# Expert slots of a mixture layer: first products two slots ahead, rows turned four ahead, slots rectified by ScalarE and VectorE in turn

## The chip, the core and the metric

The kernel runs on one core of one Trainium2 chip. The metric is the device time of one execution in microseconds (us). PE is TensorE, ACT ScalarE, DVE VectorE, POOL GpSimd, SP the engine that issues most DMAs.

## The reference

One transformer layer on x of 8 x 512 rows of 128 numbers, float32:

```
x = x + attention(layernorm(x), Wq, Wk, Wv, Wo, bo)      # 16 heads of 8, causal
h = layernorm(x).reshape(4096, 128)
probs = softmax(h @ gate_w.T)                            # 8 experts
topk_probs, topk_idx = top_k(probs, 2)
out_e = relu(h @ w1[e] + b1[e]) @ w2[e] + b2[e]          # 128 -> 512 -> 128
x = x + sum over the two chosen e of topk_probs * out_e
```

Only the two chosen experts of each row are needed.

## The kernel before, in words

Each engine has its own instruction stream, written out in full, and the streams meet at semaphores. Up to 350 us the kernel does attention, batch by batch (8 batches); beside it the finished batches are normalised a second time, routed, and scattered by POOL into `sorted_x`, a list in device memory that is sorted by expert in blocks of 128 rows.

From 350 us on the stage that is changed runs: 71 *slots* (`NSLOTS`), numbered 0 to 70. A slot is one block of 128 rows of one expert. The first 33 (`SLOTS[0]`) hold rows of batches that are routed already; slot 33 and later ones may hold rows of the last batches, whose scatters POOL issues between the slots (`SCATTERS6` in slots 1, 3, ... 13, `SCATTERS` in slots 15, 17, 18, 20, 21, 23, 24, 25). So the load of slot 33 waits until the scatter of slot 25 has landed. For slot i:

- SP: `load(i)` (L460) reads the block's number and brings the rows to `xs_t`, a ring of four (`ROUND`); it waits until PE has turned, and DVE has found the rows of, slot i-4.
- PE: `turn_xs(i)` (L1183, matmul L1187) transposes the rows into a PSUM bank; ACT: `copy_xs(i)` (L879) copies them to `xsT`; ACT: `copy_w1(i)` (L884) copies the expert's w1 to `w1_t`.
- PE: `expand(i)` (L1189, L1197), the first product, four matmuls 128x128x128 in float32; then `relu(i)`: ACT rectifies two of the four pieces (L890, L895), DVE the other two (L1737, L1743), into `hT`.
- PE: `contract(i)` (L1201, L1208), the second product, into `psO` or `psM` in turn (even and odd slots).
- DVE: `copy_y(i)` (L1747, L1750) adds b2 and writes `y_t` (named Qs in the profile); `find_rows` (L1752, L1756) works out where the rows go; POOL: `store_y(i)` (L692, L695) scatters them to `token_y` in device memory.

The order is written out by hand. In iteration i of the loops PE does expand(i+1), contract(i), turn_xs(i+3); ACT relu(i+1), copy_xs(i+3), copy_w1(i+3); DVE relu(i+1), copy_y(i), find_rows(i+2), then pieces of the last batch's attention and routing (`tail`) and weighted sums (`combine`). `xsT`, `w1_t` and `hT` have two places each, and expand uses two banks per slot, four in all. In the profile `turned` is xsT, `qrest` w1_t and `krest` hT. Near the end SP also loads results back in 512 KB pieces (`results_of`, L475 to L480), for the last two of which it waits until the scatter of slot 62 has landed; load(69) and load(70) are behind these on SP.

Of the kernel before, what the change touches and what calls it, by code (L numbers as in the profile page):

```python
# [13 lines left out]
P = 128  # L14
# [49 lines left out]
Y_RING = 8  # L64

# [77 lines left out]
def layer(nc, x, wq, wk, wv, wo, bo, gate_w, w1, b1, w2, b2, out):  # L143
    with ExitStack() as ctx:
# [134 lines left out]
        banks = [psT[:, 0, :], psT[:, 1, :], psT[:, 2, :], psS[:, 2, :]]  # L279
# [74 lines left out]
        def expert_reader(eng):  # L354
# [3 lines left out]
            def expert_of(i, at):  # L358
# [5 lines left out]
                if i not in experts:  # L364
                    experts.pop(i - 3, None)

                    experts[i] = eng.snap(words[k] // E ** (i - k * ROUND) % E, min_val=0, max_val=E - 1)
# [341 lines left out]
        def _(act):  # L709
# [169 lines left out]
            def copy_xs(i):  # L879
                act.wait_ge(xs_turned, i + 1)  # L880
                at_least(act, h_ready, i - 1)
                act.activation(xsT[:, i % 2, :], psS[:, 0, 0:P], ACT.Copy).then_inc(xsT_copied, 1)  # L882

            def copy_w1(i, e):  # L884

                at_least(act, h_ready, i - 1)
                act.activation(w1_t[:, i % 2, :], w1_sb[:, bass.ds(e, 1), :].rearrange("p a f -> p (a f)"), ACT.Copy)\  # L887
                    .then_inc(w1_copied, 1)

            def relu(i, e):  # L890

                act.wait_ge(h_ready, i + 1)
                at_least(act, y_ready, i - 1)
                for c in range(FC // 2):
                    last = act.activation(hT[:, i % 2, c * P:(c + 1) * P], banks[2 * (i % 2)][:, c * P:(c + 1) * P], ACT.Relu,  # L895
# [3 lines left out]
            act.wait_ge(moe_in, (1 + 2 * E) * 16)  # L899
            act.wait_ge(routed, 1)  # L900
# [3 lines left out]
            for i in range(2):  # L904
                copy_xs(i)
            relu(0, expert_of(0, 0))
            copy_xs(2)
            copy_w1(2, expert_of(2, 0))
# [19 lines left out]
        def _(pe):  # L928
# [254 lines left out]
            def turn_xs(i):  # L1183

                pe.wait_ge(xs_loaded[i % ROUND], (i // ROUND + 1) * 16)
                at_least(pe, xsT_copied, i)
                pe.transpose(psS[:, 0, 0:P], xs_t[:, i % ROUND, 0:D], identf[:, :]).then_inc(xs_turned, 1)  # L1187

            def expand(i):  # L1189
# [3 lines left out]
                at_least(pe, relu_act, i - 1)  # L1193
                at_least(pe, relu_dve, i - 1)
                for c in range(FC):
                    bank, c0 = banks[2 * (i % 2) + c // (FC // 2)], c % (FC // 2) * P
# [680 lines left out]
```

## Time and profile before

| | |
|---|---|
| time, median of 3 runs | 506.52 us (505.99 to 507.28) |
| span of the profiled execution | 527.7 us (no other time of that execution is given) |
| PE, PEld, DVE, ACT, POOL busy | 89%, 62%, 78%, 68%, 54% |
| chain that ended last, by engine | PE 50%, DVE 28%, ACT 7%, issue 7%, DMA 4% |
| slot stage | 350 to 516 us, then the last results and sums to 527.7 us |

PE is matmul work, PEld its weight loads, which lie beside it. A float32 matmul stands as two records, so the four matmuls of an expand are "x8" in a row. A timeline row has the start, the time from there to its end, the engine, line, operation, tiles and how many records it merges; in brackets the idle time of the engine before it and what ended it. "remote" is a semaphore event whose sender the profile could not name. The span is 21.2 us longer than the median time.

### The profile page before, as it was taken

What the parts mean: (1) busy time and instruction counts of PE and PEld (TensorE: products, weight loads), DVE (VectorE), ACT (ScalarE), POOL (GpSimd) and SP (SyncE); (2) the same over time, 40 slices, a digit from 0 to 9 for tenths busy, and PEclk for the clock granted to TensorE, in tenths of its full rate; (3) what the DMA queues carried; (4) which work ended last, traced back from release to release, by engine and by line L of the source; (5) the groups of instructions that cost most, each with busy time, mean ns of one, the idle gap of its engine ahead of it and who ended that gap; (6) DMA issues with size and microseconds to landing.
All of it is one profiled execution on the core that took longest, in us unless ns stands there. A gap on an engine that the chain in (4) does not pass through costs nothing.

```text
span 527.7 us, 14330 instructions
## 1 busy us (share of the span) xinstructions
PE 469.7 (89%) x4121; PEld 328.0 (62%) x4121; DVE 413.1 (78%) x1519; ACT 358.9 (68%) x782; POOL 286.6 (54%) x579
## 2 busy tenths in 40 slices
PE   3788999999999999999999999989788789999981
PEld 1545656556555545546555545459688679999980
DVE  6898878988988888888888897875556555557875
ACT  7576877777867867876866857875456457777750
POOL 5603544535755766657657565725456555545542
PEclk9879999999999999999999999999999899999997
DMA  7434232132233233233333326722222322235653
GB/s 225 134 93 129 56 118 91 56 118 88 67 120 108 70 108 110 76 101 97 102 95 98 106 76 175 209 65 63 56 63 69 85 77 74 71 79 180 182 172 101
DMA packets 49454, 54.92 MB, mean 104 GB/s; under 512 B 6564, under 2 KB 41554, under 8 KB 49377
## 3 DMA queue, kind: packets, MB, share of 16 engines
q1 hardware_dynamic: 44736, 45.18, 29.5%
q0 software_dynamic: 4320, 8.47, 4.7%
q8 instruction: 35, 0.57, 0.5%
q14 instruction: 43, 0.34, 0.2%
q10 hardware_dynamic: 320, 0.36, 0.2%
HBM read 34.96 MB, written 17.90 MB: 100 GB/s over the span
## 4 chain that ended last, share of the span: by engine, by line
PE 50%; DVE 28%; ACT 7%; issue 7%; DMA 4%; another core or an unknown queue 3%; ACTq 1%; SPq 0%; POOL 0%; DVEq 0%; POOLq 0%
PE psO L1035 12%; DVE psS L1349 10%; PE psT L1197 7%; DVE maxs L1352 7%; PE psS L998 7%; PE psM L1208 5%; PE psO L1208 5%; PE psT L1011 3%; PE psS L1197 2%; ACT PT L811 2%; DMA xs_t<-sorted_x 2%; PE psS L1187 2%; DVE maxs L1349 1%; DVE xn L1278 1%
## 5 line engine op out<-in xcount | busy, mean ns | idle before, releaser
L811 ACT ACTIVATE PT<-psT 128x512 f32<-128x512 f32 x320 | 172.5, 594 | 67.6 <-PE psO L1035 45.0
L1349 DVE CUSTOM_DVE_ANT_0 psS<-mask_row,psS 128x512 f32<-128x512 bf16 (+1 forms) x232 | 142.8, 624 | 33.6 <-PE psS L998 29.3
L998 PE MATMUL psS<-Ks,Qs 96*128 96x128 bf16 (+3 forms) x512 | 132.9, 308 | 9.5 <-DVE maxs L1352 7.3
L598 POOL TENSOR_SCALAR_AFFINE_SELECT PT<-PT 128x512 f32<-128x512 f32 x124 | 76.8, 635 | 96.0 <-ACT PT L811 94.8
L1011 PE MATMUL psT<-Qs,Ks 108*128 108x384 bf16 (+3 forms) x512 | 109.9, 299 | 4.2 <-ACT PT L811 3.0
L695 POOL DMA_INDIRECT token_y<-Qs,y_row x71 | 70.8, 997 | 74.6 <-DVE Qs L1750 39.0
L998 PEld LDWEIGHTS psS<-Ks,Qs 96*128 96x128 bf16 x512 | 50.4, 99 | 53.5 <-DVE maxs L1352 26.4
L629 POOL DMA_INDIRECT sorted_x<-xn,place x64 | 64.3, 1005 | 27.6 <-issue 16.5
L1352 DVE TENSOR_REDUCE maxs<-psS 128x2 f32<-128x512 f32 (+3 forms) x120 | 75.7, 669 | 1.8 <-PE psS L1001 1.4
L1035 PE MATMUL psO<-PT,Vs 128*32 128x512 f32 (+3 forms) x1024 | 75.8, 436 | 0.3 <-DVE x_all L1375 0.3
L1011 PEld LDWEIGHTS psT<-Qs,Ks 108*128 108x128 bf16 x512 | 43.5, 97 | 32.8 <-ACT PT L811 12.9
L1197 PE MATMUL psT<-turned,qrest 128*128 128x128 f32 x428 | 61.0, 280 | 1.3 <-ACT qrest L887 0.9
L895 ACT ACTIVATE krest<-psT,turned 128x128 f32<-128x128 f32 x142 | 44.7, 365 | 25.7 <-PE psT L1197 8.1
L1197 PEld LDWEIGHTS psT<-turned,qrest 128*128 128x128 f32 x428 | 54.1, 194 | 2.6 <-issue 2.5
L1035 PEld LDWEIGHTS psO<-PT,Vs 128*32 128x32 f32 x1024 | 28.6, 109 | 40.9 <-issue 27.4
L1001 PE MATMUL psS<-mask_row,identb 128*128 128x128 bf16 x280 | 49.9, 226 | 0.0
L887 ACT ACTIVATE qrest<-w_sb 128x512 f32 x71 | 44.6, 630 | 0.4 <-issue 0.4
L882 ACT ACTIVATE turned<-psS 128x128 f32<-128x128 f32 x71 | 19.7, 278 | 35.5 <-PE psS L1187 17.0
L1208 PE MATMUL psO<-w_sb,krest 128*128 x288 | 40.4, 285 | 3.4 <-ACT krest L895 2.3
L1208 PE MATMUL psM<-w_sb,krest 128*128 x280 | 38.2, 279 | 5.7 <-ACT krest L895 3.1
L1743 DVE TENSOR_SCALAR krest<-psS,turned 128x128 f32<-128x128 f32 x70 | 21.5, 347 | 23.0 <-PE psS L1197 12.1
L1208 PEld LDWEIGHTS psO<-w_sb,krest 128*128 128x128 f32 x288 | 36.6, 199 | 4.5 <-issue 4.4
(260 smaller groups left out, 741.1 us busy)
## 6 DMA issues: line engine op xcount, KB each, us to landing
Qs<-q_parts SPq DMA_DIRECT2D x96, 96.0 KB
Ks<-k_parts SPq DMA_DIRECT2D x95, 96.0 KB
xs_t<-sorted_x SPq DMA_DIRECT2D x71, 65.0 KB
w_sb<-in_L_ffn_w SPq DMA_DIRECT2D x16, 256.0 KB
k_parts<-kparts SPq DMA_DIRECT2D x8, 384.0 KB, 2.6
q_parts<-qparts SPq DMA_DIRECT2D x8, 384.0 KB, 3.6
x_all<-in_L_attn_x SPq DMA_DIRECT2D x8, 256.0 KB, 4.7
v_all<-token_y SPq DMA_DIRECT2D x4, 512.0 KB, 4.4
```

Of the source, the lines that this page charges most:

```text
L598: pool.affine_select(out=square, in_=square, compare_op=ALU.is_ge, fill=0.0, base=0, pattern=[[0, GH], [1, P]], channel_multiplier=-1).the ...
L629: pool.indirect_dma_start(out=xs_dram, out_offset=bass.IndirectOffsetOnAxis(ap=place[:, b, k, c:c + 1], axis=0), in_=xn2[:, b * CH + c, :] ...
L695: pool.indirect_dma_start(out=token_y, out_offset=bass.IndirectOffsetOnAxis(ap=y_row[:, i % (2 * Y_RING):i % (2 * Y_RING) + 1], axis=0), i ...
L811: act.activation(PT[:, n * T:(n + 1) * T], psT[:, bank, :], ACT.Exp).then_inc(prob_done[bank], 1)
L998: last = pe.matmul(psS[:, bank, c0:c0 + n], Qs[0:QK_ROWS, g, h, j * P:n], Ks[0:QK_ROWS, g, h, 0:n], start=True, stop=alone)
L1001: last = pe.matmul(psS[:, bank, c0 + n - P:c0 + n], identb[:, :], mask_qk[:, :], start=False, stop=True)
L1011: last = pe.matmul(psT[:, bank, c0:c0 + T - i * P], Ks[0:ST_ROWS, g, h, i * P:(i + 1) * P], Qs[0:ST_ROWS, g, h, i * P:T], start=True, stop ...
L1035: last = pe.matmul(psO[h * VW:(h + 1) * VW, i * P:T], Vs[:, g, i, h, :], PT[:, c0:c0 + cols], start=(i == KEY_BLOCKS[0]), stop=(i == KEY_B ...
L1197: last = pe.matmul(bank[:, c0:c0 + P], w1_t[:, i % 2, c * P:(c + 1) * P], xsT[:, i % 2, :], start=True, stop=True)
L1208: last = pe.matmul(ps_v[i % 2][:, 0:D], hT[:, i % 2, c * P:(c + 1) * P], w2_sb[:, bass.ds(e, 1), c, :].rearrange("p a d -> p (a d)"), star ...
L1349: dve.tensor_tensor_reduce(src, mask_row[:, (CH - 1 - j) * P:], src, 1.0, NEG, ALU.add, ALU.max, maxs[:, par, j, h:h + 1]).then_inc(scores ...
L1352: dve.tensor_reduce(maxs[:, par, j, h:h + heads], src, AX_X, ALU.max).then_inc(scores_used[bank], 1)
```

## The change

`expand` runs two slots ahead of `contract` instead of one, and `turn_xs` four ahead instead of three. `w1_t` and `hT` get three places (`DEEP`), in the memory of `qparts` and `kparts`; `xsT` gets four (`X_DEEP`), in that of `xn`. A slot's first product takes one whole bank of `psT` (three in turn) instead of two half banks of four; the turned rows use two banks in turn. Even slots are rectified by ACT alone and odd ones by DVE alone, four pieces each. The order of ACT's work in an iteration changes: copy_w1(i+3), relu(i+2) if i is even, copy_xs(i+4). DVE does relu(i+2) if i is odd, copy_y(i), find_rows(i+3). SP's and POOL's instructions are the same as before.

```diff
-        xsT = turned[:, E + E * FC:].rearrange("p (n d) -> p n d", n=2)
+        xsT = xn[:, 0, :, :]
-        w1_t = qrest
-        hT = krest
+        w1_t, hT = (v[:, :, :, :].rearrange("p u a t -> p (u a t)").bitcast(F32).rearrange("p (n f) -> p n f", n=DEEP)
+                    for v in (qparts, kparts))
-        banks = [psT[:, 0, :], psT[:, 1, :], psT[:, 2, :], psS[:, 2, :]]
+        xs_bank = [psS[:, 0, 0:P], psS[:, 2, 0:P]]
...
 # ACT
             def copy_xs(i):
                 act.wait_ge(xs_turned, i + 1)
-                at_least(act, h_ready, i - 1)
+                at_least(act, h_ready, i - X_DEEP + 1)
...
             def relu(i, e):
                 act.wait_ge(h_ready, i + 1)
-                at_least(act, y_ready, i - 1)
-                for c in range(FC // 2):
+                at_least(act, y_ready, i - DEEP + 1)
+                for c in range(FC):
...
-                if i + 1 < NSLOTS:
-                    relu(i + 1, expert_of(i + 1, i))
                 if i + 3 < NSLOTS:
-                    copy_xs(i + 3)
                     copy_w1(i + 3, expert_of(i + 3, i))
+                if i + 2 < NSLOTS and i % 2 == 0:
+                    relu(i + 2, expert_of(i + 2, i))
+                if i + 4 < NSLOTS:
+                    copy_xs(i + 4)
...
 # PE
             def turn_xs(i):
                 pe.wait_ge(xs_loaded[i % ROUND], (i // ROUND + 1) * 16)
-                at_least(pe, xsT_copied, i)
+                at_least(pe, xsT_copied, i - 1)
...
+            def rectified(i):
+                pe.wait_ge((relu_act, relu_dve)[i % 2], i // 2 + 1)
             def expand(i):
                 pe.wait_ge(xsT_copied, i + 1)
                 pe.wait_ge(w1_copied, i + 1)
-                at_least(pe, relu_act, i - 1)
-                at_least(pe, relu_dve, i - 1)
+                if i >= DEEP:
+                    rectified(i - DEEP)
...
-                if i + 1 < NSLOTS:
-                    expand(i + 1)
+                if i + 2 < NSLOTS:
+                    expand(i + 2)
                 contract(i, expert_of(i, i))
-                if i + 3 < NSLOTS:
-                    turn_xs(i + 3)
+                if i + 4 < NSLOTS:
+                    turn_xs(i + 4)
...
 # DVE
-                if i + 1 < NSLOTS:
-                    relu(i + 1, expert_of(i + 1, i))
+                if i + 2 < NSLOTS and i % 2:
+                    relu(i + 2, expert_of(i + 2, i))
                 copy_y(i, expert_of(i, i))
-                if i + 2 < NSLOTS:
-                    find_rows(i + 2)
+                if i + 3 < NSLOTS:
+                    find_rows(i + 3)
```

On PE, the begin of the slots up to the first contract; before (L1187 turns, L1197 expands, L1208 contracts; ISA rows compute addresses):

```order
L1187 MATMUL psS<-identf,xs_t 128x128 x2
L1197 MATMUL psT<-turned,qrest 128x128 x4
L1187 MATMUL psS<-identf,xs_t 128x128
L1197 MATMUL psT<-turned,qrest 128x128 x2
L1197 MATMUL psS<-turned,qrest 128x128 x2
L363 TENSOR_LOAD turns
L363 ISA x2
L1208 ISA
L1208 MATMUL psO<-w_sb,krest 128x128
```

and now (L1194 turns, L1207 expands, L1217 contracts):

```order
L1194 MATMUL psS<-identf,xs_t 128x128 x2
L1207 MATMUL psT<-xn,qparts 128x128 x4
L1194 MATMUL psS<-identf,xs_t 128x128
L1207 MATMUL psT<-xn,qparts 128x128 x4
L1194 MATMUL psS<-identf,xs_t 128x128
L1207 MATMUL psT<-xn,qparts 128x128 x4
L365 TENSOR_LOAD turns
L365 ISA x2
L1217 ISA
L1217 MATMUL psO<-w_sb,kparts 128x128
```

Three expands and four turns now stand ahead of the first contract, where there were two and three. From there on each iteration has the same three groups, one slot further on for expand and turn.

On ACT, one iteration inside the slots before (L882 copy_xs, L887 copy_w1, L895 rectify):

```order
L895 ISA
L895 ACTIVATE krest<-psT,turned 128x128
L895 ISA
L895 ACTIVATE krest<-psT,turned 128x128
L882 ACTIVATE turned<-psS 128x128
L887 ISA
L887 ACTIVATE qrest<-w_sb 128x512
```

and two iterations now (L884 copy_xs, L889 copy_w1, L897 rectify; `qparts` is w1_t, `kparts` hT, `xn` xsT):

```order
L884 ACTIVATE xn<-psS 128x128
L889 ISA
L889 ACTIVATE qparts<-w_sb 128x512
L884 ACTIVATE xn<-psS 128x128
L889 ISA
L889 ACTIVATE qparts<-w_sb 128x512
L897 ISA
L897 ACTIVATE kparts<-psT,turned 128x128
L897 ISA
L897 ACTIVATE kparts<-psT,turned 128x128
L897 ISA
L897 ACTIVATE kparts<-psT,turned 128x128
```

A fourth piece follows. The four pieces of an even slot stand ahead of the next copy_xs; in the other iteration ACT has the two copies alone.

## Rows read from the trace of the kernel before

**Rows 1.** Stretches (span, busy us of each engine with counts, granted clock, DMA share, GB/s).

```profile
386.00:418.00 32.00, 25.19 (x208) 23.56 (x207) 18.38 (x83) 17.09 (x52) 19.04 (x19) 1.00 0.27 75
430.00:505.00 75.00, 74.14 (x650) 72.95 (x649) 49.97 (x193) 55.13 (x153) 38.65 (x40) 1.00 0.39 110
```

**Rows 2.** Timeline of PE, one slot of the even stretch.

```profile
438.67 0.27 PE L1187 MATMUL psS<-identf,xs_t 128*128 128x128 f32 x1
...
439.67 1.06 PE L1208 MATMUL psO<-w_sb,krest 128*128 x8
440.56 0.27 PE L1187 MATMUL psS<-identf,xs_t 128*128 128x128 f32 x1
```

**Rows 3.** Timeline of all engines there: ACT, DVE and POOL.

```profile
443.78 0.63 ACT L895 ACTIVATE krest<-psT,turned 128x128 f32<-128x128 f32 x2 [0.18 <-PE psS L1197]
443.91 0.61 DVE L1743 TENSOR_SCALAR krest<-psS,turned 128x128 f32<-128x128 f32 x2 [0.72 <-PE psS L1197]
...
444.67 0.29 DVE L1750 TENSOR_TENSOR Qs<-psO,b_b 128x128 f32<-128x128 f32 x1
444.67 0.28 ACT L882 ACTIVATE turned<-psS 128x128 f32<-128x128 f32 x1 [0.26 <-PE psS L1187]
...
445.73 0.98 POOL L695 DMA_INDIRECT token_y<-Qs,y_row  x1 [0.91 <-issue]
```

**Rows 4.** Timelines of PE: contract(0), contract(25), and the turn of slot 33.

```profile
355.03 1.15 PE L1208 MATMUL psO<-w_sb,krest 128*128 x8 [0.19 <-issue]
...
423.33 1.15 PE L1208 MATMUL psM<-w_sb,krest 128*128 x8
...
436.69 0.27 PE L1187 MATMUL psS<-identf,xs_t 128*128 128x128 f32 x1
```

**Rows 5.** Timeline of all engines around contract(9).

```profile
375.63 1.13 PE L1197 MATMUL psT<-turned,qrest 128*128 128x128 f32 x8
...
378.78 0.63 ACT L895 ACTIVATE krest<-psT,turned 128x128 f32<-128x128 f32 x2 [3.75 <-remote]
378.93 0.61 DVE L1743 TENSOR_SCALAR krest<-psS,turned 128x128 f32<-128x128 f32 x2 [3.68 <-remote]
...
379.84 1.15 PE L1208 MATMUL psM<-w_sb,krest 128*128 x8 [3.08 <-ACT krest L895]
```

**Rows 6.** Stretch after that gap.

```profile
382.00:384.00 2.00, 2.00 (x11) 2.00 (x11) 0.80 (x3) 0.63 (x2) 1.49 (x2) 0.50 0.34 103
```

**Rows 7.** Timeline of all engines around contract(21).

```profile
409.71 0.61 DVE L1743 TENSOR_SCALAR krest<-psS,turned 128x128 f32<-128x128 f32 x2 [1.12 <-issue]
...
410.63 1.15 PE L1208 MATMUL psM<-w_sb,krest 128*128 x8 [1.16 <-issue]
```

**Rows 8.** POOL's last scatter, then a chain's DMA, SP's load(33), the first load and turn.

```profile
428.07 0.99 POOL L695 DMA_INDIRECT token_y<-Qs,y_row  x1 [1.82 <-DVE Qs L1750]
429.37 0.97 POOL L629 DMA_INDIRECT sorted_x<-xn,place  x1 [0.30 <-issue]
...
480.63 2.29 DMA token_y<-Qs,y_row
...
433.28 0.34 SPq L473 DMA_DIRECT2D xs_t<-sorted_x  x1
...
L473 SPq DMA_DIRECT2D xs_t<-sorted_x x71: 15/338/722, 349.4 to 505.9; - x71
...
351.30 0.30 PE L1187 MATMUL psS<-identf,xs_t 128*128 128x128 f32 x1 [0.35 <-DMA xs_t<-sorted_x]
```

**Rows 9.** End of contract(62) (next turn), load(70) in the chain, its turn, contract(70).

```profile
499.10 0.27 PE L1187 MATMUL psS<-identf,xs_t 128*128 128x128 f32 x1
...
505.94 4.92 DMA xs_t<-sorted_x
...
510.90 0.33 PE L1187 MATMUL psS<-identf,xs_t 128*128 128x128 f32 x1 [1.34 <-DMA xs_t<-sorted_x]
...
515.38 1.15 PE L1208 MATMUL psO<-w_sb,krest 128*128 x8 [0.39 <-issue]
```

More of the change, by code:

```diff
@@ L64 @@
 Y_RING = 8
+DEEP = 3
+X_DEEP = 4
 TAIL = dict(heads=0, norm=0, sorted6=1, attention=1, copy_attention=1, project=2, add=2, keep=4, best=4, second=5,
@@ L892, in relu @@
                 act.wait_ge(h_ready, i + 1)
-                at_least(act, y_ready, i - 1)
-                for c in range(FC // 2):
-                    last = act.activation(hT[:, i % 2, c * P:(c + 1) * P], banks[2 * (i % 2)][:, c * P:(c + 1) * P], ACT.Relu,
+                at_least(act, y_ready, i - DEEP + 1)
+                for c in range(FC):
+                    last = act.activation(hT[:, i % DEEP, c * P:(c + 1) * P], psT[:, i % DEEP, c * P:(c + 1) * P], ACT.Relu,
                                           bias=b1T[:, bass.ds(e * FC + c, 1)])
@@ L899, in _ @@
             act.wait_ge(moe_in, (1 + 2 * E) * 16)
+            act.wait_ge(q_stored[1], BATCH // 2 * Q_STORES)
+            act.wait_ge(k_stored[1], BATCH // 2 * K_STORES)
             act.wait_ge(routed, 1)
@@ L903, in _ @@
             copy_heads(STEPS - 1, GROUPS - 1)
-            for i in range(2):
+            for i in range(3):
                 copy_xs(i)
-            relu(0, expert_of(0, 0))
-            copy_xs(2)
-            copy_w1(2, expert_of(2, 0))
+                if i == 0:
+                    copy_w1(2, expert_of(2, 0))
+                if i == 1:
+                    relu(0, expert_of(0, 0))
+            copy_xs(3)
             for i in range(NSLOTS):
@@ L1185, in turn_xs @@
                 pe.wait_ge(xs_loaded[i % ROUND], (i // ROUND + 1) * 16)
[L1186 to L1187 removed]
+                at_least(pe, xsT_copied, i - 1)
+                pe.transpose(xs_bank[i % 2], xs_t[:, i % ROUND, 0:D], identf[:, :]).then_inc(xs_turned, 1)
+            def rectified(i):
+                pe.wait_ge((relu_act, relu_dve)[i % 2], i // 2 + 1)
             def expand(i):
@@ L1192, in expand @@
                 pe.wait_ge(w1_copied, i + 1)
-                at_least(pe, relu_act, i - 1)
-                at_least(pe, relu_dve, i - 1)
+                if i >= DEEP:
+                    rectified(i - DEEP)
                 for c in range(FC):
-                    bank, c0 = banks[2 * (i % 2) + c // (FC // 2)], c % (FC // 2) * P
-                    last = pe.matmul(bank[:, c0:c0 + P], w1_t[:, i % 2, c * P:(c + 1) * P], xsT[:, i % 2, :],
-                                     start=True, stop=True)
+                    last = pe.matmul(psT[:, i % DEEP, c * P:(c + 1) * P], w1_t[:, i % DEEP, c * P:(c + 1) * P],
+                                     xsT[:, i % X_DEEP, :], start=True, stop=True)
                 last.then_inc(h_ready, 1)
@@ L1203, in contract @@
                     pe.wait_ge(heads_copied, STEPS)
-                pe.wait_ge(relu_act, i + 1)
-                pe.wait_ge(relu_dve, i + 1)
+                rectified(i)
                 at_least(pe, y_copied, i - 1)
                 for c in range(FC):
-                    last = pe.matmul(ps_v[i % 2][:, 0:D], hT[:, i % 2, c * P:(c + 1) * P],
+                    last = pe.matmul(ps_v[i % 2][:, 0:D], hT[:, i % DEEP, c * P:(c + 1) * P],
                                      w2_sb[:, bass.ds(e, 1), c, :].rearrange("p a d -> p (a d)"),
@@ L1218, in _ @@
             turn_xs(2)
+            expand(1)
+            turn_xs(3)
             for i in range(NSLOTS):
@@ L1739, in relu @@
                 dve.wait_ge(h_ready, i + 1)
-                at_least(dve, y_ready, i - 1)
-                for c in range(FC // 2, FC):
-                    c0 = (c - FC // 2) * P
-                    last = dve.tensor_scalar(hT[:, i % 2, c * P:(c + 1) * P], banks[2 * (i % 2) + 1][:, c0:c0 + P],
+                at_least(dve, y_ready, i - DEEP + 1)
+                for c in range(FC):
+                    last = dve.tensor_scalar(hT[:, i % DEEP, c * P:(c + 1) * P], psT[:, i % DEEP, c * P:(c + 1) * P],
                                              b1T[:, bass.ds(e * FC + c, 1)], 0.0, ALU.add, ALU.max)
@@ L1835, in _ @@
             dve.wait_ge(routed, 1)
-            find_rows(0)
-            find_rows(1)
-            relu(0, expert_of(0, 0))
+            dve.wait_ge(k_stored[1], BATCH // 2 * K_STORES)
+            for i in range(3):
+                find_rows(i)
+            relu(1, expert_of(1, 0))
             summed = 0
```

8 lines of the change are left out of this document (4 added, 4 removed).

## The prediction, made before the changed kernel was run

> **What bounds the kernel now.** I read the stretches first, then PE's timeline, then who waited for whom inside the gaps. The reader is to see two regimes in one loop. In the even stretch, 430 to 505 us, PE is busy 74.14 of 75 us [rows 1]: a slot is a turn, an expand and a contract, and turns follow each other after 440.56 - 438.67 = 1.89 us, of which a contract is 440.56 - 439.67 = 0.89 [rows 2]. ACT, DVE and POOL have time to spare [rows 3]. PE's work per slot is the same after the change, so nothing is gained there. In the other stretch, from the first slot to about 432 us, PE is busy only 25.19 of 32 us in the piece shown [rows 1]. Contract(25) starts 423.33 - 355.03 = 68.3 us after contract(0) [rows 4]. 25 slots at 1.89 are 47.3; the last batch's turns, projections and count take about 2 (four groups of four matmuls, each half an expand, 0.45 [rows 2], and the count). **Some 19 us are lost**, and the change can only win from these.
>
> What are the gaps? The largest is at contract(9) [rows 5]. PE's expand(10) starts at 375.63 and should end at 376.7. ACT and DVE, which need the products, wake at 378.78 and 378.93, after 3.75 and 3.68 us, for an event without a sender, though the expand(9) that they rectify was earlier still. PE idles 3.08 us until both have rectified. So PE's signals arrive late by up to 4 us, and PE runs out of work that it may do without them. After it the granted clock is 0.50, which is 1.2 GHz, in 382 to 384 [rows 6]. By distances of contract starts above 1.89, the losses are: before contract 4 1.2, 7 1.3, 9 3.4, 10 and 11 1.7 (half clock), 14 2.0, 16 0.7, 17 1.8, 21 1.4, 22 0.9, 24 3.2, 25 1.0 (half clock): 18.6. Of these 17 and 21 are of another kind: at 21 DVE started its half of the rectifying 1.12 us late behind its own work, and PE waited 1.16 [rows 7].
>
> The Trainium skill, "TensorE: Matmul & The Clock Gate", section "HAM oscillation — how this bites in real kernels", says that a long wait of TensorE puts it back to half clock, so that the gap is paid twice. The trace agrees: 0.50 stands right behind the 3.08 us of idle time. By that rule a gap that becomes short gives its slow stretch back entirely; by my sum only half of it comes back.
>
> **The change part by part.**
>
> *Deeper first product.* When signals stop, PE could before run at most the next expand and the next contract. After, relu(i) was signalled a slot earlier, so one more contract, 0.89 us [rows 2], is possible; not a whole slot more, since the expand after it needs copy_xs of rows whose turn is not signalled either, and the contract after it copy_y. Below, the gain of a gap can be nothing (if it is freed by the slower rectifying, next item); above, a whole slot, 1.89. I take 0.9 for the seven gaps of over 1 us (4, 7, 9, 14, 17, 21, 24) and all of the two small ones: 7 x 0.9 + 1.6 = 7.9.
>
> *One engine rectifies four pieces.* Two take 0.63 on ACT, 0.61 on DVE [rows 3], the second 0.27 after the first; four are 0.35 + 3 x 0.27 = 1.16. That is 0.55 longer for a slot, and as much work over two slots. In the even stretch it is hidden by the additional slot. After a late signal it is not: ACT must do relu(i+2) before copy_xs(i+4) when i is even, which then frees PE. Half of nine gaps pay 0.55: +2.5.
>
> *Half clock.* 2.7 us are lost to it. The two gaps that caused it shrink from some 3 us by one; I take half back: 1.4. Slots 0 to 25 in sum: -7.9 + 2.5 - 1.4 = **-6.8**.
>
> *Begin.* PE does a third expand and a fourth turn before contract(0), which starts about 1.3 us later, but with that expand done: 0. The new waits for `q_stored` and `k_stored` are for DMAs of the attention stage: 0. The moved copy_w1 waits for an expand two slots back: 0.
>
> *Rows are needed one slot sooner.* This is the part that costs. The ring of `xs_t` still has four places, so in the ring itself load and turn move together. But two loads come at a time that something else sets. (a) load(33) waits for the scatter of slot 25. A POOL scatter costs 429.37 - 428.07 = 1.30 [rows 8]. From slot 15 to 25 POOL has 11 stores and 8 scatters, 19 x 1.3 = 24.7 us, in ten slots of PE, 18.9; so its last scatter starts about 4.9 us after copy_y(25) even without a late signal. Then landing (2.29 in the chain), SP's issue, landing of the load (first load 349.4, first turn 351.30: 1.9) [rows 8]: 4.2 at least, 5.8 by this execution (433.28 + 1.9 - 429.37). Turn(33) is possible 0.5 + 4.9 + 4.2 to 5.8 = 9.6 to 11.2 us after contract(25). PE wants it after five slots, 9.5, before, and after four, 7.6, now. If the chain decides in both, the cost is a whole slot, **+1.9**. In the profiled execution it came at 433.28 + 1.9 = 435.2, 11.0 after contract(25) ended (424.2), and PE only wanted it at 436.69 [rows 4, 8], having lost 3.0 to late signals by then. There the loss becomes 11.0 - 7.6 = 3.4, **+0.4**. (b) load(70), behind the results' loads, lets turn(70) start 510.90 - 499.10 = 11.8 us after contract(62), the load itself taking 4.92 [rows 9]. PE wants it after 9.5 now and waited 2.3, and 0.5 more for relu(70) ahead of contract(70) at 515.38. After, it wants it at 7.6 and waits 4.2, with contracts left to fill the end: 4.2 + 0.2 against 2.8 is +1.5; the earlier start of some loads takes 0.4 of it: **+1.1**. (c) find_rows stands behind four pieces instead of two in odd slots, so some loads go out 0.3 later; at one or two slots after 475 us, where loads are slow, that shows: **+0.3**.
>
> On the scale of the profiled execution: -6.8 + 0.4 + 1.1 + 0.3 = -5.0, a span of 522.7.
>
> **From the span to the runs.** The span is 527.7, the median 506.52: 21.2 us more. No stretch has idle time of that size but the slots up to 432. So some of the late signals may be missing in timed runs. Without them the gains that stay are contract 17 and 21 and small ones, some 3 us; the cost of (a) is 1.9: -3.0 + 1.9 + 1.1 + 0.3 = +0.3. Between -5.0 and +0.3 I choose the middle, -2.4: **504.1, say 504 us**. Its own range is 501.5 to 505.5.
>
> **The rivals.**
>
> A. *The late signals belong to the recording.* The 21.2 us and the 19 lost us are near enough. For it: in the even stretch nothing of this kind is lost, although PE is busier. Against it: the late signals begin and end with the scatters of rows to `sorted_x`, which run in any execution. Time: 506.52 + 0.3 = 506.8. The Trainium skill, "NOTIFIC — the notification-queue block", section 7.1, says that the block which writes trace records holds back its producers inside rather than lose a record, and that this can stall an engine. By this rule the gain of the deeper buffers would exist in the profile alone; that this happens here no row shows.
>
> B. *The rows' arrival decides; slower.* Place: turn(33) and turn(70), which PE now wants a slot earlier than their loads can land. Price: 1.9 + 1.5, and 0.4 at the slow loads around 480 to 490. With gains of about 1, if ACT's order (relu before copy_xs) eats the depth: 506.52 + 2.8 = 509.3. It decides from the point where turn(33) can come later than 7.6 us after contract(25); rows 8 say 9.6 at least, so the wait itself is nearly certain, only its cover is not.
>
> C. *The depth hides nearly all.* If the signals are late for both kinds of run and a gap shrinks by a whole slot, 1.9, below what lowers the clock: 7 x 1.9 + 1.6, cut to the gap's size 12, + 2.7 of clock, - 1.8: 506.5 - 8 = 498.5 (of the -13, the part in timed runs). Against it: the chain through copy_xs and copy_y above.
>
> D. *The change doesn't deepen anything*, since copy_y and copy_xs stop PE at the same point as before: then 0 gained and (a) to (c): it counts with B.
>
> **Chances.** Forecast 0.45, A 0.25, B and D 0.20, C 0.10. A measurement of this kernel tells 0.3%, 1.5 us, from no change: 505.0 to 508.0 is the same. The forecast is faster in 0.40 and same in 0.05; A is faster 0.04, same 0.17, slower 0.04; B slower; C faster. Faster 0.54, same 0.22, slower 0.24. The range goes from C's time to B's: 498.5 to 509.0.
>
> **What would show it.** In the profile after: the even stretch still 1.89 per slot; the loss from contract(0) to contract(25) down from 19 to about 12; before turn(33) an idle time of PE that ends with a DMA to `xs_t`, of 1 to 3 us; before the turns of slots 69 and 70 waits of about 4 together; relu in groups of four, 1.16 us, on ACT and DVE in turn. I am wrong if the loss in slots 0 to 25 does not fall, if it falls by more than 10, or if turn(33) does not wait. If the span falls by 5 and the timed runs do not move, A holds.

## The result, and the profile of the changed kernel

Beside each other on one chip the kernel before took 506.9 us (median of 4 runs, 505.99 to 507.62) and the changed kernel 510.06 us (4 runs, 509.04 to 511.44): ratio 1.006, 95% interval 1.0038 to 1.0083. A repetition on chip 11 gave 509.7 against 507.03 us, 1.0049 (1.0028 to 1.0071). **The change makes the kernel 2.7 to 3.2 us, 0.5 to 0.6%, slower**; 504 us was forecast.

One thing has to be known for all that follows. The kernel before was timed on six occasions, each on one chip, and its median was 506.9, 507.03 and 507.27 us on three of them and 531.64, 532.35 and 536.37 on the others, with nothing in between. I call these chips of the fast and of the slow kind; each occasion had a chip of its own, so the runs can't tell the chip from the occasion. (Two of the 23 executions of before on the last chip took 602 and 665 us at a granted clock of 0.74 and 0.66, and are in no ratio.) The profile ahead of the prediction (span 527.7, late signals) is of the second kind, the times beside it are of the first. The changed kernel was profiled on a chip of the first kind: span 506.9 us in an execution of 509.04. So its rows must not be set against the rows of before, but against a second profile of the kernel before on a chip of the first kind (span 503.9, time 505.7), called *the quiet profile of before* here. Comparisons are only made within a kind. The ratios are those on record, and can differ from the quotient of two medians by up to 0.3%.

The changed kernel's page, the span and the busy times:

```profile
span 506.9 us, 14197 instructions
...
PE 461.7 (91%) x4121; PEld 326.5 (64%) x4121; DVE 408.1 (81%) x1517; ACT 352.9 (70%) x784; POOL 285.5 (56%) x579
```

What PE waited for between 345 and 520 us (total us, times, longest), first in the quiet profile of before, then in the changed kernel:

```profile
PE psS L1187 <- DMA xs_t<-sorted_x: 2.0, 3, 1.2
PE psM L1208 <- ACT krest L895: 2.0, 2, 1.2
PE psS L1187 <- ACT turned L882: 0.9, 1, 0.9
PE psM L1208 <- issue: 0.7, 1, 0.7
PE psO L1208 <- issue: 0.6, 2, 0.4
```

```profile
PE psS L1194 <- DMA xs_t<-sorted_x: 8.0, 8, 1.7
PE psT L1207 <- issue: 0.3, 1, 0.3
```

This is the whole result in seven rows. Every wait for ACT or DVE is gone, as a deeper pipeline promises (in the repetition one of 0.2 us is left). In their place PE waits for rows, four times as long as before: 8.0 us, in the repetition 7.7. Of the 8.0 us 1.2 stand before the first two turns, 3.6 before those of slots 26, 28 and 33, and 3.2 before those of slots 66, 69 and 70. And the 3.08 us gap with half clock behind it [rows 5, 6] is in neither: on this kind of chip the signals aren't late, and the granted clock is 1.00 in all slots of both profiles.

Where the new waits stand, PE's timeline of the changed kernel (the second row is the turn of slot 28, the sixth the turn of slot 33, after them slots 66, 69 and 70):

```profile
400.62 1.06 PE L1217 MATMUL psO<-w_sb,kparts 128*128 x8
403.30 0.33 PE L1194 MATMUL psS<-identf,xs_t 128*128 128x128 f32 x1 [1.62 <-DMA xs_t<-sorted_x]
403.46 1.07 PE L1207 MATMUL psT<-xn,qparts 128*128 128x128 f32 x8
404.36 1.06 PE L1217 MATMUL psM<-w_sb,kparts 128*128 x8
...
412.24 1.06 PE L1217 MATMUL psM<-w_sb,kparts 128*128 x8
414.96 0.33 PE L1194 MATMUL psS<-identf,xs_t 128*128 128x128 f32 x1 [1.66 <-DMA xs_t<-sorted_x]
...
479.11 0.33 PE L1194 MATMUL psS<-identf,xs_t 128*128 128x128 f32 x1 [0.90 <-DMA xs_t<-sorted_x]
...
486.14 0.33 PE L1194 MATMUL psS<-identf,xs_t 128*128 128x128 f32 x1 [1.11 <-DMA xs_t<-sorted_x]
...
489.42 0.33 PE L1194 MATMUL psS<-identf,xs_t 128*128 128x128 f32 x1 [1.15 <-DMA xs_t<-sorted_x]
```

The turn of slot 33 answers to the 436.69 of [rows 4], which didn't wait. It comes four slots behind contract(25), at 404.36, and waits as the prediction said. That of slot 28 was not foreseen. One part of it stands in SP's queue (L426 writes pad rows for the last batch's list, one expert in each of the iterations 16 to 23):

```profile
397.43 0.34 SPq L475 DMA_DIRECT2D xs_t<-sorted_x  x1
398.58 0.35 SPq L426 DMA_DIRECT2D sorted_x<-pad_row  x1
399.77 0.34 SPq L475 DMA_DIRECT2D xs_t<-sorted_x  x1
400.88 0.35 SPq L426 DMA_DIRECT2D sorted_x<-pad_row  x1
402.07 0.34 SPq L475 DMA_DIRECT2D xs_t<-sorted_x  x1
403.18 0.36 SPq L426 DMA_DIRECT2D sorted_x<-pad_row  x1
```

A load and a clear together take SP 399.77 - 397.43 = 2.34 and 402.07 - 399.77 = 2.30 us, where PE's slot takes 1.90. SP falls behind by 0.4 us in each iteration, and PE, which now wants the rows a slot sooner, catches up with it: the rows of slot 19 landed at 381.44, 1.8 us before their turn (383.26), those of slot 26 at 397.61, 0.05 before theirs (397.66). From there on a load that is late is waited for in full. The load of slot 28 is the row of 399.77, and it was late: a load raises its semaphore 16 times, and in this trace 15 of the 16 had come by 401.95, the last at 403.25, while PE was ready at 403.30 - 1.62 = 401.68. So SP's pace alone made some 0.3 us of this wait, and one late sixteenth the other 1.3. The profile of the repetition has no wait at slot 28, but waits of 0.65, 0.49 and 0.27 us at slots 23, 29 and 30 (at slot 23 again by one late sixteenth, 391.40 after 389.66 for the other 15): the places change from run to run, the missing reserve is in both. What makes a sixteenth late no run shows.

A third cost stands behind the last product. POOL's timeline there, of the quiet profile of before (contract(70) starts at 491.81) and of the changed kernel (at 494.21):

```profile
490.84 0.98 POOL L695 DMA_INDIRECT token_y<-Qs,y_row  x1 [2.48 <-DVE Qs L1750]
492.63 0.98 POOL L695 DMA_INDIRECT token_y<-Qs,y_row  x1 [0.80 <-DVE Qs L1750]
494.18 0.99 POOL L695 DMA_INDIRECT token_y<-Qs,y_row  x1 [0.57 <-issue]
```

```profile
493.02 0.98 POOL L697 DMA_INDIRECT token_y<-Qs,y_row  x1 [2.43 <-DVE Qs L1760]
494.65 0.98 POOL L697 DMA_INDIRECT token_y<-Qs,y_row  x1 [0.64 <-issue]
495.93 1.11 POOL L697 DMA_INDIRECT token_y<-Qs,y_row  x1 [0.30 <-DVE Qs L1760]
497.35 0.99 POOL L697 DMA_INDIRECT token_y<-Qs,y_row  x1 [0.30 <-issue]
```

The last store starts 494.18 - 491.81 = 2.37 us after contract(70) before, and 497.35 - 494.21 = 3.14 now. With the last expand done a slot earlier, the last contracts follow each other after 0.89 and 1.05 us, but a store takes POOL 1.28 to 1.42, so they queue: +0.8 us behind contract(70).

The slots of both quiet profiles, in us between starts of contracts:

| | before | changed |
|---|---|---|
| turn(0) to contract(0) | 3.68 | 5.00 |
| contract 0 to 30 | 63.85 | 64.38 |
| contract 30 to 50 | 37.99 | 37.92 |
| contract 50 to 70 | 40.49 | 40.16 |
| contract(70) to the end of the span | 12.1 | 12.7 |

That is +2.1 us from turn(0) to the end. The spans differ by 3.0, since turn(0) itself was 0.95 us later in this execution; in the profile of the repetition it was not (345.89 against 345.80), and there the sum is +2.5.

### The profile page after: what moved, and what is told of

The parts are those of the page before. It is cut to its first block, busy times and chain, and to the rows that moved or that the text cites. A ratio compares the mean times of both kernels' runs of the same rounds, so it can differ in the third digit from the quotient of the medians.

```text
span 506.9 us, 14197 instructions
## 1 busy us (share of the span) xinstructions
PE 461.7 (91%) x4121; PEld 326.5 (64%) x4121; DVE 408.1 (81%) x1517; ACT 352.9 (70%) x784; POOL 285.5 (56%) x579
## 4 chain that ended last, share of the span: by engine, by line
PE 54%; DVE 30%; issue 5%; DMA 4%; ACT 4%; SPq 1%; DVEq 1%; POOL 1%; ACTq 0%; POOLq 0%
PE psO L1042 14%; DVE psS L1360 10%; PE psT L1207 9%; PE psS L1005 8%; DVE maxs L1363 7%; PE psO L1217 5%; PE psM L1217 4%; PE psT L1018 3%; DMA xs_t<-sorted_x 2%; ACT PT L813 2%; DVE maxs L1360 2%; PE psM L1052 1%; PE psS L1194 1%; PE psS L1008 1%; DVE attn L1374 1%
## 5 line engine op out<-in xcount | busy, mean ns | idle before, releaser
L813 ACT ACTIVATE PT<-psT 128x512 f32<-128x512 f32 x320 | 172.3, 597 | 69.3 <-PE psO L1042 46.7
L1207 PE MATMUL psT<-xn,qparts 128*128 128x128 f32 x568 | 75.5, 276 | 0.5 <-issue 0.3
L1207 PEld LDWEIGHTS psT<-xn,qparts 128*128 128x128 f32 x568 | 69.0, 192 | 1.2 <-issue 0.5
L1753 DVE TENSOR_SCALAR kparts<-psT,turned 128x128 f32<-128x128 f32 x140 | 39.6, 344 | 15.4 <-PE psT L1207 11.6
L889 ACT ACTIVATE qparts<-w_sb 128x512 f32 x71 | 45.3, 639 | 8.0 <-issue 8.0
L897 ACT ACTIVATE kparts<-psT,turned 128x128 f32<-128x128 f32 x144 | 40.9, 365 | 7.0 <-PE psT L1207 7.0
L884 ACT ACTIVATE xn<-psS 128x128 f32<-128x128 f32 x71 | 20.1, 284 | 35.4 <-PE psS L1194 35.4
L1217 PE MATMUL psO<-w_sb,kparts 128*128 x288 | 38.4, 276 | 0.0
L1217 PE MATMUL psM<-w_sb,kparts 128*128 x280 | 37.0, 275 | 0.0
L1760 DVE TENSOR_TENSOR Qs<-psO,b_b 128x128 f32<-128x128 f32 x36 | 10.5, 291 | 32.2 <-PE psO L1217 28.5
```

Source lines behind the costliest of these rows:

```text
L813: act.activation(PT[:, n * T:(n + 1) * T], psT[:, bank, :], ACT.Exp).then_inc(prob_done[bank], 1)
L1207: last = pe.matmul(psT[:, i % DEEP, c * P:(c + 1) * P], w1_t[:, i % DEEP, c * P:(c + 1) * P], xsT[:, i % X_DEEP, :], start=True, stop=True)
L1217: last = pe.matmul(ps_v[i % 2][:, 0:D], hT[:, i % DEEP, c * P:(c + 1) * P], w2_sb[:, bass.ds(e, 1), c, :].rearrange("p a d -> p (a d)"), s ...
```

## The experiments

First a second look at the kernel before, on a chip of the slow kind (before: 531.64 us).

*b0_again*: the kernel before, unchanged.

> The kernel before, unchanged, profiled once more. The profile of before that was read had a span 21 us over the median, with signals of TensorE up to 4 us late; the changed kernel's had a span 2 us under its time and none. Theory 'that one execution was disturbed': span about 505, contract(0) to contract(25) about 51 us instead of 68, no wait that ends with an event without a sender. Rival 'the late signals belong to the kernel before': span about 527 again. In either case it shows how long TensorE waits for rows before the turns of slots 28, 33 and 66 to 70: I expect under 4 us in all, against 6.8 in the changed kernel.

Measured: 535.08 us, span 533.3. The signals are late here again: contract 0 to 30 takes 83.28 us, in the profile ahead of the prediction 80.77, in the quiet profile 63.85. The time is that of the whole execution and it is long too, as are the 17 runs of before without a profile (529.14 to 535.26). **So the late signals do not belong to the recording; as far as the six occasions show, they go with the chip or the occasion.** Rival A fell with it, and so did the reading that one execution was disturbed.

*b0_third*: the same kernel on a chip of the fast kind (before: 507.27 us).

> The kernel before, once more, for a profile where its signals are not late (if the chip is such a one: its median near 507). Theory 'rows' arrival': TensorE waits for rows 2 to 4 us in all, against 6.8 in the changed kernel, hardly any before slots 25 to 34; contract(0) to contract(30) takes about 60 to 62 us, against 64.4. Rival: before has the same waits, and the difference lies elsewhere.

Measured: 505.7 us, span 503.9, no late signal; contract 0 to 30 takes 63.85 us, not 60 to 62. It is the quiet profile used above.

**What each part of the change does.** *e_alt* keeps the memory, the banks and the taking in turn of the changed kernel, but sets the distances back to those of before:

```diff
-            expand(1)
-            turn_xs(3)
...
-                    expand(i + 2)
+                    expand(i + 1)
...
-                    turn_xs(i + 4)
+                    turn_xs(i + 3)
```

(ACT and DVE accordingly: relu(i+1), copy_xs(i+3), find_rows(i+2).)

> The changed kernel with the distances of before: expand one slot ahead, turns three ahead, and the order of ScalarE and VectorE in an iteration as before; the rectifying in turn, the single banks and the new places of the buffers stay. Theory 'rows' arrival' (turns four ahead want rows before SP can bring them): as fast as before, 506.9 within 1. Rival 'rectifying by one engine costs' : it keeps the loss, 509 to 510.5, or more, since a slot's 1.16 us on one engine now has one slot less of cover.

*e_turn4* is that with turns, copy_xs and find_rows again as far ahead as in the changed kernel:

```diff
-                    turn_xs(i + 3)
+                    turn_xs(i + 4)
...
-                    find_rows(i + 2)
+                    find_rows(i + 3)
```

> As the kernel with the old distances, but turns, copies of rows and find_rows one slot further ahead as in the change (four ahead); expand stays one ahead. Theory 'rows' arrival': the loss comes back with this alone, 509 to 510.5, and TensorE's waits for rows in the profile are 5 to 8 us. Rival 'rectifying by one engine': no difference to the kernel with old distances.

Both ran twice, the second time (*e_alt2*, *e_turn4b*) on a chip of the fast kind:

> The same kernel as e_alt (distances of before, rectifying in turn), to be compared where signals are not late. Theory 'rows' arrival': 506.5 to 508 where before takes 507. Rival 'rectifying by one engine costs': 509 to 511. If the chip has late signals again: 1.01 of before, as the first time.

> The same kernel as e_turn4 (turns four ahead, expand one ahead, rectifying in turn). Theory 'rows' arrival': 2 to 3.5 us slower than the same kernel with turns three ahead, with waits for rows of 6 to 8 us. Rival: no difference between the two.

Measured, ratio to before on the same chip:

| | slow kind | fast kind |
|---|---|---|
| in turn, old distances | 1.0112 (1.0069 to 1.0155) | 1.0103 (1.0073 to 1.0133), 512.53 us |
| and turns four ahead | 1.0162 (1.0118 to 1.0205) | 1.0172 (1.0141 to 1.0202), 515.3 us |
| and expand two ahead (the changed kernel) | not run | 1.0049 to 1.006, 509.7 us |

The expectation that the old distances bring back the time of before was wrong, its rival held. So on the fast kind: one engine for four pieces costs +5.3 us, turning earlier (with copy_xs and find_rows) +2.8, and only expanding earlier wins: about -5.4, the difference between +8.0 and +2.7, which were measured on two chips (-4.9 with the first comparison's +3.2). It pays back what the taking in turn costs and not much more. The +5.3 is strictly that of the taking in turn together with the new banks and places of the buffers, which e_alt keeps; no run parts them. What speaks for the rectifying are PE's waits of e_alt2 (then of e_turn4b), 345 to 520 us:

```profile
PE psM L1214 <- DVE kparts L1748: 6.3, 9, 1.5
PE psS L1191 <- DMA xs_t<-sorted_x: 1.7, 3, 0.7
PE psO L1214 <- ACT kparts L897: 1.4, 3, 0.6
```

```profile
PE psS L1193 <- DMA xs_t<-sorted_x: 6.2, 7, 1.8
PE psM L1216 <- DVE kparts L1751: 5.3, 8, 1.3
```

In the quiet profile of before no wait ends with DVE; here nine do. Where DVE is late with its own work, four pieces of one engine end later than two. In e_alt2 a reduction of the last batch's routing is in DVE's way:

```profile
393.63 1.10 DVE L1612 TENSOR_REDUCE blockf<-past 128x38 f32<-128x912 f32 x1
...
395.95 1.13 DVE L1748 TENSOR_SCALAR kparts<-psT,turned 128x128 f32<-128x128 f32 x4 [1.00 <-PE psO L1214]
...
397.32 1.15 PE L1214 MATMUL psM<-w_sb,kparts 128*128 x8 [1.32 <-DVE kparts L1748]
```

The reduction ends at 394.73, 0.6 us after the expand that DVE is to rectify (393.04 + 1.06 = 394.10). The 1.00 us of idle time behind it is longer. (The contract that is named for it had ended at 395.0, since it ran 1.06 us from 393.94; what DVE waited for after that the profile doesn't show.) The last two rows of waits say where the turning costs: waits for rows go from 1.7 to 6.2 us with turns alone moved. Most of the growth of that wait comes from the turns; the expands add the rest, to 7.7 and 8.0.

Two-ahead expands with both engines on every slot were not tried. The kernel before gives each engine a bank of its own for its two pieces, two banks per slot; three slots at a time would want six, and the changed kernel uses five for expands and turned rows together. Whether the depth can be had without the taking in turn no run tells.

**Whether the waits for rows are what is lost.** Three edits of tables on the changed kernel are each aimed at one.

*a_again*: the changed kernel once more, for the comparison (before on this chip: 507.03 us).

> The changed kernel, unchanged. On the chip of the last runs the kernel before takes 531.6 us and TensorE's signals are up to 4 us late in its slots; on the chip of the first times it takes 506.9. Theory 'rows' arrival' holds for undisturbed signals: where before takes 505 to 508, the ratio is 1.004 to 1.008. Where signals are late, my forecast said that depth pays: ratio under 1. Rival 'depth does not shorten the wait for a late signal, since the copy of the rows behind four rectified pieces is what TensorE waits for': ratio 1.008 to 1.015 there.

Measured: 509.7 us, 1.0049 (1.0028 to 1.0071). *e_scat*, *e_clear* and *e_all* ran on the same chip, so they are compared with this run.

*e_scat* puts the last batch's scatters earlier, for the wait at slot 33:

```diff
-SCATTERS = {slot: number for number, slot in enumerate((15, 17, 18, 20, 21, 23, 24, 25))}
+SCATTERS = {slot: number for number, slot in enumerate((15, 16, 17, 18, 19, 20, 21, 22))}
```

> The changed kernel with the last batch's scatters on GpSimd in slots 15 to 22 instead of 15 to 25. Theory 'rows' arrival': the wait before the turn of slot 33 (1.7 us) goes, since the last scatter starts 2 to 3 us earlier; 1 to 2 us faster than the changed kernel. Rival: the wait is SP's, not the scatter's, and stays.

Measured: 508.44 us, 1.0023 (0.9999 to 1.0046): 1.3 us won over a_again, which is less than the two intervals can tell apart. The wait at slot 33 is gone, those for rows in all went from 7.7 to 5.2 us.

*e_clear* spreads SP's clears, for the wait at slot 28:

```diff
-CLEARS = {16 + e: (e,) for e in range(E)}
+CLEARS = {slot: (e,) for e, slot in enumerate((16, 17, 19, 20, 22, 23, 25, 26))}
```

> The changed kernel with SP's eight clears of padding rows spread over iterations 16 to 26 instead of one in each of 16 to 23. In the changed kernel's profile SP needs 2.3 us for a load and a clear against 1.9 us of a slot, and TensorE waits 1.6 us before the turn of slot 28. Theory 'rows' arrival': that wait goes, the wait before the turn of slot 33 (1.7 us) stays or grows by up to half a microsecond; 0.5 to 1.8 us faster than the changed kernel. Rival (the wait is slack that comes back before slot 33): same as the changed kernel within 0.5.

Measured: 509.78 us, 1.0054 (1.0032 to 1.0076): nothing. PE's turns of slots 28, 29 and 33, first in a_again, then in e_clear:

```profile
401.24 0.33 PE L1194 MATMUL psS<-identf,xs_t 128*128 128x128 f32 x1
403.85 0.33 PE L1194 MATMUL psS<-identf,xs_t 128*128 128x128 f32 x1 [0.49 <-DMA xs_t<-sorted_x]
...
414.24 0.33 PE L1194 MATMUL psS<-identf,xs_t 128*128 128x128 f32 x1 [1.70 <-DMA xs_t<-sorted_x]
```

```profile
401.26 0.27 PE L1194 MATMUL psS<-identf,xs_t 128*128 128x128 f32 x1
403.93 0.33 PE L1194 MATMUL psS<-identf,xs_t 128*128 128x128 f32 x1 [0.58 <-DMA xs_t<-sorted_x]
...
414.85 0.33 PE L1194 MATMUL psS<-identf,xs_t 128*128 128x128 f32 x1 [1.92 <-DMA xs_t<-sorted_x]
```

On this chip there was no wait at slot 28 to take away. The waits of slots 23 to 30 are 1.4 us in all in a_again and 1.0 in e_clear, and what is won there is waited at slot 33: its turn comes 63.2 us after contract(0) in the changed kernel, 63.3 in a_again and 63.5 in e_clear, but 61.1 in e_scat. The chain through the scatters sets that moment.

*e_tail* loads the results of batches 5 and 6 two iterations of SP later, so that they are no longer ahead of load(69) and load(70):

```diff
-RESULTS = [SLOT_ENDS[0] + n for n in (1, 3, 6, 9, 12)] + [SLOT_ENDS[1] + n for n in (-1, 0)]
+RESULTS = [SLOT_ENDS[0] + n for n in (1, 3, 6, 9, 12)] + [SLOT_ENDS[1] + n for n in (1, 2)]
```

> The changed kernel with SP's loads of results of batches 5 and 6 two iterations later, behind the loads of slots 69 and 70 instead of ahead of them. Theory 'rows' arrival': the waits before the turns of slots 69 and 70 (2.3 us in the profile, 3.2 with that of slot 67) shrink to under 1; time 507.5 to 508.5. Rival: the results now come late for VectorE's sums, and the time stays 509.5 to 511.

It was run on three chips, all of the slow kind.

> The changed kernel with the results of batches 5 and 6 loaded two iterations of SP later, so that they are no longer ahead of load(69) and load(70). In the changed kernel's trace of an undisturbed chip the turns of slots 69 and 70 wait 1.11 and 1.15 us, contract(66) and contract(67) are 1.35 and 1.38 late. Theory (the tail's waits are on the path, term (b)): these go, 2.0 to 2.5 us faster than the changed kernel, ratio to the kernel before about 1.001. Rival (the later results end later and the final sums wait for them): no change against the changed kernel, 1.005 to 1.006.

> The changed kernel with only the results of batches 5 and 6 loaded two iterations of SP later, hoped for on a chip whose signals are not late (a time of the kernel before near 507 us). Theory (term (b) of the tail is on the path): ratio to the kernel before about 1.001, 2.0 to 2.5 us faster than the changed kernel. Rival (the last sums wait longer in its place): 1.005 to 1.006.

Measured: 1.0079 (1.0054 to 1.0105), 1.0042 (1.0010 to 1.0074) and 1.0029 (1.0002 to 1.0056). In all seven traces of the changed kernel with this edit contract 66 to 70 takes 5.65 or 5.66 us and nothing waits there; in the changed kernel's two profiles without the edit it is 7.00 and 6.21. What it brings alone on the fast kind stays open.

*e_all* makes all three edits.

> The changed kernel with all three: clears spread, scatters in slots 15 to 22, the results of batches 5 and 6 loaded two iterations later. Theory 'rows' arrival': TensorE's waits for rows fall from 6.8 to under 2 us and the time to 504.5 to 506.5 where before takes 506.9, so at or below it. Rival 'rectifying by one engine costs': it stays above 508.

Measured: **505.49 us, 0.9954 (0.9932 to 0.9975), faster than both kernels** on the one chip of the fast kind where it ran (by the medians 1.5 us or 0.30% faster than before). Span 503.3, waits for rows 4.3 us. It wins 4.2 us on a_again, and the profiles say where: contract 0 to 30 takes 63.26 us in place of 64.49, and contract 50 to 70 takes 37.80 in place of 40.58. The second stretch, 2.8 us, is that of the third edit (each figure is from one execution). The waits for rows were expected under 2 us.

The spread clears are in the way here. The turn of slot 33 still waits 0.80 us in e_all, though the last scatter had landed at 407.52, 4 us before the load. SP's queue and SP's wait from 408 to 413 us:

```profile
408.70 0.35 SPq L426 DMA_DIRECT2D sorted_x<-pad_row  x1
411.58 0.34 SPq L475 DMA_DIRECT2D xs_t<-sorted_x  x1
...
SPq L127 <- DMA sorted_x<-pad_row: 1.1, 1, 1.1
```

load(33) also waits until all clears have landed, and the edit moves the last one from iteration 23 to 26, right ahead of it.

*b_all* makes the same three edits on the kernel before.

> The kernel before with the three edits of e_all (clears spread, scatters in slots 15 to 22, results of batches 5 and 6 loaded two iterations later). It wants rows one slot later, so the theory 'rows' arrival' gives it less: its waits for rows of 2 to 4 us shrink, 504.5 to 506 where before takes 507, level with e_all within 0.5 us. If e_all's own gain comes from the deeper first product, b_all stays 1 us or more above e_all.

Measured: 506.78 us against 507.27, 1.0000 (0.9978 to 1.0021). Its waits between 345 and 520 us:

```profile
PE psM L1208 <- ACT krest L895: 3.5, 3, 1.5
...
PE psS L1187 <- DMA xs_t<-sorted_x: 0.3, 1, 0.3
```

The rows are there in time (2.0 us of waits before, 0.3 now), and nothing is won, against the expectation. ACT is late in their place (3.5 us in place of 2.0). Contract 0 to 30 and 50 to 70 are 0.9 and 0.7 us shorter than in the quiet profile, but contract 30 to 50 is 1.0 longer, just behind the turn of slot 33, whose load waits for the last spread clear as in e_all (1.2 us in SP's queue), and the end behind contract(70) is 0.8 longer. So two other costs stand beside rectifying, and one may be the clears' own. **With these three edits depth and earlier supply are worth more together than apart**: 505.49 to 507.03 with both, 1.0000 with the supply alone, 1.005 with the depth alone. Whether a supply without the spread clears would help the kernel before too was not run.

*e_sr* leaves the clears out of e_all; *e_all2* is e_all again beside it.

> The changed kernel with the scatters of the last batch in slots 15 to 22 and the results loaded later, without the spread clears. Theory (SP's clears cost nothing by themselves, but once turn(33)'s wait is gone theirs decides): about 1.4 us slower than with all three edits, ratio to the kernel before 0.998. Rival (clears cost nothing in any combination): as with all three, 0.995.

> All three edits on the changed kernel, again, to compare the other two on one chip. Expected as before: ratio 0.995 to the kernel before. If this chip's signals from TensorE are late the ratio will be near 1.004 instead.

> The changed kernel with scatters in slots 15 to 22 and results later, clears as they were, on the same chip. Where signals are not late, theory (clears decide once the scatters are out of the way): ratio 0.998, against 0.995 with all three edits. Rival (clears cost nothing in any combination): 0.995.

All three fell on chips of the slow kind (before 532.35 and 536.37 us): e_sr 1.0002 (0.9975 to 1.0028), e_sr2 0.9985 (0.9956 to 1.0014), e_all2 1.0038 (1.0009 to 1.0066). The chip with 532.35 us had both e_sr (532.78 us) and e_all2 (534.90): the kernel without the spread clears is the faster by 2.1 us, the opposite of what was expected, though the two intervals overlap. In e_all2 the turn of slot 33 waits 1.10 us and SP waits for a clear as in e_all, in e_sr and e_sr2 it doesn't wait. So the spread clears probably cost; for the fast kind this was not run. The gain of e_all was seen on one chip of the fast kind alone.

**What the depth does where signals are late.** The changed kernel itself was not run there, e_tail comes next to it. Its stretches (first row), then its timeline at a long gap and the stretch behind it:

```profile
350.00:432.00 82.00, 66.81 (x543) 62.24 (x540) 45.47 (x202) 42.20 (x125) 39.35 (x40) 0.94 0.24 66
```

```profile
391.24 0.27 PE L1194 MATMUL psS<-identf,xs_t 128*128 128x128 f32 x1
...
392.69 1.14 ACT L897 ACTIVATE kparts<-psT,turned 128x128 f32<-128x128 f32 x4 [3.58 <-remote]
394.15 0.28 ACT L884 ACTIVATE xn<-psS 128x128 f32<-128x128 f32 x1 [0.33 <-remote]
...
394.32 0.29 DVE L1760 TENSOR_TENSOR Qs<-psO,b_b 128x128 f32<-128x128 f32 x1 [4.36 <-remote]
...
394.89 0.26 ACT L884 ACTIVATE xn<-psS 128x128 f32<-128x128 f32 x1
...
395.09 2.05 PE L1207 MATMUL psT<-xn,qparts 128*128 128x128 f32 x8 [3.57 <-ACT xn L884]
...
395.00:397.10 2.10, 2.01 (x9) 2.04 (x10) 1.86 (x11) 0.67 (x2) 0.98 (x1) 0.50 0.20 54
```

And the same stretch of b0_again, one expand ahead:

```profile
350.00:432.00 82.00, 66.71 (x542) 60.72 (x539) 46.83 (x203) 43.70 (x125) 41.06 (x41) 0.96 0.25 66
```

PE is busy 66.8 and 66.7 of 82 us: the depth fills no gap. The timeline says why. ACT, which has waited 3.58 us for its event, must first rectify four pieces (1.14), then make two copies of rows with one of w1 between, and only the copy of 394.89 lets the next expand go. That expand takes 2.05 us in place of 1.06, in a stretch with a granted clock of 0.50, 1.2 GHz, behind 3.57 us of idle time, as [rows 5, 6] had it. On this chip contract 0 to 25 takes 70.87 us in e_tail, 71.35 in e_turn4 (one expand ahead), 70.80 in e_alt and 69.66 in b0_again. These are single executions, but a gain of 6.8 us would show. Contract 0 to 30 takes 86.86, 86.16 and 85.57 us in the three profiles of e_tail, against 80.77 and 83.28 in the two of before.

## Why the prediction was wrong, by its own steps

**The failed step is "deeper first product": "the gain of a gap ... I take 0.9 for the seven gaps of over 1 us ... 7 x 0.9 + 1.6 = 7.9", and what hangs on it, -6.8 for slots 0 to 25.** It failed twice.

1. The gaps were read from a profile of another kind of chip than the times. "Some of the late signals may be missing in timed runs" was seen, from a span 21.2 us above the median, but taken as half the case, and -5.0 and +0.3 were averaged. On the chips of the given times all were missing. The branch without them was the one to forecast: a span longer than every run's time says that the profile is not of these runs.
2. Where the signals are late the gain doesn't exist either. Contract 0 to 25 takes 69.3 to 70.9 us in the three profiles of e_tail against 68.3 and 69.7 of before, not 6.8 less (contract 0 to 30 is 2 to 6 us longer). The prediction's own sentence had the reason: ACT must do relu(i+2) before copy_xs(i+4). But it was priced at 0.55 us for half the gaps, where the row shows 1.14 plus the copies in line, 394.89 + 0.26 - 392.69 = 2.46 us between ACT's event and PE's.

*One engine rectifies four pieces.* Duration right: 1.16 forecast, 1.12 to 1.14 measured. Cost: +2.5 forecast for late signals, and nothing without them; measured apart from the depth, with the banks and places, it is +5.3 us on the fast kind (nine waits for DVE), a kind of wait that was only seen at contract 17 and 21. The deeper expand hides it.

*Half clock.* No stretch of the slots is at half clock on the fast kind, so nothing to give back.

*Begin, 0.* Right: contract(0) 1.3 us later, and about 1.0 less work behind contract(50).

*(a) turn(33), +1.9.* Right in place and size: 1.66 us of wait at 414.96, 9.5 us after contract(25) ended (9.6 to 11.2 forecast), and e_scat removes it. *The ring itself, 0*: wrong. "In the ring itself load and turn move together" holds only while SP keeps pace. With a clear per iteration it takes 2.3 us, the reserve is gone by slot 26, and the turns of slots 23 to 30 wait 2.0 us in one profile (most of it one late sixteenth of a load) and 1.4 in the other. As e_clear shows, less waiting there gives nothing while the wait of slot 33 stands.

*(b) tail, +1.1, and (c), +0.3.* Forecast together +1.4. Contract 50 to 70 is 0.3 us shorter, but has 1.0 less of PE's work: +0.7, in the repetition +1.1. The place was right (slots 66, 69, 70). The sum of (b) has a slip: 4.2 + 0.2 against 2.8 is +1.6, not +1.5.

*Missed: the end behind contract(70), +0.6*, POOL's queue of stores. I had looked at what each engine does per slot, not at what follows when the last slots come at 0.89 us.

In the forecast's branch without late signals stood -3.0 + 1.9 + 1.1 + 0.3 = +0.3. With 1.6 for the ring (turn(28)) and 0.6 for the end it would have been +2.5; the two quiet comparisons give +2.1 and +2.5, the times +2.7 and +3.2. The -3.0 was sound: the waits of the quiet profile other than for rows are 4.2 us, and all but 0.3 are gone.

*The rivals.* B, "the rows' arrival decides", 509.3 us, is what happened, in mechanism and nearly in time, with one place more (turn(28)) and without ACT's order having to eat the depth on the fast kind. It was given 0.20, and its 509.3 us lie outside the stated range, which ends at 509.0. A was nearer to the measured time than the forecast, for a wrong reason: the signals are late in runs without a recording too. The Trainium skill, "NOTIFIC — the notification-queue block", section 7.1, says that writing trace records can hold an engine up; no run here bears that out for these gaps. C fell with the gain. D is half true on the fast kind: the depth does remove waits (-5.4 us), but not those for late signals.

## What to carry to other kernels

Before anything is forecast from a profile, set its span against the times of the runs: where it is longer than all of them, find the idle time that makes the difference and leave it out. Deepening a pipeline moves each consumer nearer to its supplier: follow every supply up to the queue that sets its pace (here SP's, 2.3 us per iteration for a load and a clear against 1.9 of a slot), and move the supply in the same change; here depth alone cost 0.5%, supply alone gave nothing, and both together won 0.3 to 0.5% on the one chip of the fast kind where they ran. Look too at what else a moved transfer holds up: the clears, spread to spare SP, ended right ahead of a load that waits for them. And where a depth is bought by giving one engine the work of two, measure that trade apart: it cost 5.3 us and the depth gave back 5.4.

## What the runs showed of the hardware

The same kernel takes 507 us on some chips and 532 to 536 on others. Contract 0 to 30 takes 80.77 and 83.28 us there against 63.85, so 17 to 19 us of it lie in these slots, where ACT and DVE sit idle for up to 4.4 us until an event whose sender the profile can't name (3.75, 3.68, 3.58 and 4.36 in the rows shown); contract(0) starts 5.6 to 8.6 us later (355.03 and 358.10 against 349.48). A stretch at 1.2 GHz (granted clock 0.50) follows the gaps of 3.08 and 3.57 us that are shown. A load of rows can have one of its 16 parts late: 1.3 us behind the other 15 at slot 28. What delays the signals was not found out. From contract 30 to 50, where no rows are scattered to `sorted_x`, the kernel before takes 38.00, 37.99 and 37.99 us in its three profiles, of either kind.
